# Transposed attention scores from high and low fp16 parts of query and key, with the low part subtracted on GpSimd

## The reference

```python
h = rms_norm(layernorm(x), norm_weight)          # x is [32, 256, 128]
q, k, v = split(h @ w_qkv.T, 3)                  # 16 heads of 64
q, k = apply_rope(q), apply_rope(k)
k = concat([persist_mem, k], axis=2)             # 4 keys in front: 260
v = concat([persist_mem, v], axis=2)
scores = einsum('bhid,bhjd->bhij', q, k) * dim_head ** -0.5
attn = softmax(where(causal, scores, min), -1)
x = x + einsum('bhij,bhjd->bhid', attn, v) @ w_out.T
c = in_c                                         # [256, 128]
for xt in layernorm(x):                          # 32 steps, one sequence each
    f, i = sigmoid(xt @ wf.T + c @ uf.T + bf), sigmoid(xt @ wi.T + c @ ui.T + bi)
    c = f * c + i * tanh(xt @ wc.T + c @ uc.T + bc)
out = x + tanh(layernorm(x) @ wo.T + c @ uo.T + bo)
```

## Time and profile before

| | before |
|---|---|
| median of 3 runs | 1352.43 us |
| lowest and highest | 1346.96 and 1360.31 us |
| profiled execution, its own time | 1353.34 us |
| profiled execution, its span | 1351.6 us |
| instructions in the span | 38016 |
| mean granted clock of TensorE | 0.958 |
| TensorE matmul, weight load | 88%, 64% of the span busy |
| VectorE, ScalarE, GpSimd | 75%, 46%, 45% |

### The profile page before, as it was taken

One profiled execution on the slowest core, in us unless ns is written; L12 is line 12 of the kernel. 1 busy time (PEld: TensorE's weight loads), 2 busy tenths in 40 slices (PEclk: granted clock), 3 DMA queues, 4 the chain that ended last, 5 costly groups with the idle time before them and its releaser, 6 DMA issues.

```text
span 1351.6 us, 38016 instructions
## 1 busy us (share of the span) xinstructions
PE 1185.7 (88%) x13841; PEld 868.7 (64%) x13841; DVE 1008.0 (75%) x3415; ACT 625.3 (46%) x1305; POOL 612.1 (45%) x948
## 2 busy tenths in 40 slices
PE   2799999999999999999999999999999999999950
PEld 1467766676776666667666666766666766667640
DVE  3767878787787877778787777877777887787426
ACT  2455444444554544545444454544445454454412
POOL 2445444444454444445444444544444454444204
PEclk9799999999999999999999999999999999999965
DMA  8222333333222323322332332223233322332114
...
DMA packets 72554, 122.63 MB, mean 91 GB/s; under 512 B 12593, under 2 KB 27442, under 8 KB 72242
## 3 DMA queue, kind: packets, MB, share of 16 engines
...
...
## 4 chain that ended last, share of the span: by engine, by line
PE 42%; DMA 18%; DVE 17%; SPq 9%; issue 7%; POOL 4%; ACT 2%; POOLq 0%; DVEq 0%; ACTq 0%
DMA rope_c<-rope_b 12%; PE bank L845 8%; PE bank_pv L935 7%; DVE masked L657 6%; DMA linv_scratch<-linv 5%; PE bank_sum L969 5%; PE bank_sum L952 5%; SPq L258 5%; PE bank_st L898 4%; DVE linv L673 4%; POOL qk L348 3%; PE bank_sm L875 3%; PE bank L861 2%; SPq L243 2%; DVE rope_b L647 2%
## 5 line engine op out<-in xcount | busy, mean ns | idle before, releaser
L348 POOL TENSOR_TENSOR qk<-rope_a,rope_c 128x512 f32<-128x512 f32 x256 | 325.5, 1272 | 413.0 <-DMA rope_c<-rope_b 392.3
L657 DVE CUSTOM_DVE_ANT_0 masked<-bank_sm,mask_q 128x132 bf16<-128x132 f32 (+1 forms) x1024 | 307.4, 356 | 42.8 <-PE bank_sm L875 42.8
L646 DVE TENSOR_TENSOR rope_a<-bank,cos 128x512 f32<-128x512 f32 x256 | 174.6, 682 | 181.4 <-PE bank L845 127.3
L466 ACT ACTIVATE prob<-bank_st 128x776 f32<-128x776 f32 x256 | 208.4, 814 | 158.4 <-PE bank_st L901 157.7
L935 PE MATMUL bank_pv<-prob,v_sb 128*64 128x256 f32 (+1 forms) x2048 | 229.5, 345 | 52.4 <-ACT raw L489 51.4
L451 ACT ACTIVATE qk_h<-qk 128x512 f16<-128x512 f32 x256 | 159.4, 623 | 208.3 <-POOL qk L348 208.1
L898 PE MATMUL bank_st<-qk 64*128 64x256 f32 (+1 forms) x2048 | 240.3, 327 | 0.0
L339 POOL TENSOR_SCALAR_AFFINE_SELECT prob<-prob 128x256 f32<-128x256 f32 x256 | 113.8, 444 | 262.6 <-ACT prob L466 262.3
L935 PEld LDWEIGHTS bank_pv<-prob,v_sb 128*64 128x64 f32 x2048 | 128.9, 137 | 123.5 <-POOL prob L341 55.1
L898 PEld LDWEIGHTS bank_st<-qk 64*128 64x128 f32 x2048 | 155.1, 188 | 31.7 <-issue 1.1
L647 DVE TENSOR_TENSOR rope_b<-bank,sin 128x512 f32<-128x512 f32 x256 | 173.8, 679 | 0.0
...
## 6 DMA issues: line engine op xcount, KB each, us to landing
rope_c<-rope_b SPq DMA_DIRECT2D x512, 128.0 KB, 2.1
rinv<-linv_scratch SPq DMA_DIRECT2D x128, 256.0 KB, 4.5
...
v_sb<-pm_v SPq DMA_DIRECT2D x64, 8.0 KB
...
```

What stands on the lines that cost most here:

```text
L348: G.tensor_tensor(qk[:, s, :].rearrange("p (u n) -> p u n", u=2)[:, :, 0:NT], rope_a[:, s % 4, :].rearrange("p (u n) -> p u n", u=2), rope ...
L466: A.activation(prob[:, s % 4, :, :], ps_st[:, :, 0:SCOL], ACT.Exp).then_inc(S["exp_done"], 1)
L646: V.tensor_tensor(rope_a[:, s % 4, :], ps_proj[:, :], cos[:, :], ALU.mult)
L657: ins = V.tensor_tensor_reduce(masked[:, e, c0:c0 + n], ps_sm[:, e, c0:c0 + n], mask_q[:, c0:c0 + n], 1.0, LOWEST, ALU.add, ALU.max, top[: ...
```

## The change

The transposed scores are no longer one fp32 product but three fp16 ones, (high, high), (high, low) and (low, high), as the projections are already. `qk_h` is there already; its partner `qk_l` is new, the difference of `qk` and `qk_h` in fp16. GpSimd subtracts it in the new `low`, for pair s-2 behind `causal` of turn s (for the last two pairs in turns 0 and 1 of the next iteration). `qk` shrinks to four buffers: `rope_add` waits for `low` of four pairs before, no longer for the scores of the batch before, and ScalarE's cast now waits for these scores. The keys of persistent memory get a low part once, in VectorE's prologue. `k_end` becomes two tiles, `k_end_h` and `k_end_l`, copied one behind the other, and `end_keys` moves from turns 1 and 6 to turns 3 and 7.

```diff
--- before.py
+++ after.py
@@ -109,11 +109,13 @@
 
 
 
-        qk = sb("qk", [P, NPAIR, 2 * NKEY], f32)
-        k_end = sb("k_end", [P, NPAIR * NEND], f32)
+        qk = sb("qk", [P, 4, 2 * NT], f32)
+        k_end_h = sb("k_end_h", [P, NPAIR * NEND], f16)
+        k_end_l = sb("k_end_l", [P, NPAIR * NEND], f16)
         top_t = sb("top_t", [P, 2, NT], bf16)
 
         qk_h = sb("qk_h", [P, NPAIR, 2 * NKEY], f16)
+        qk_l = sb("qk_l", [P, NPAIR, 2 * NKEY], f16)
         v_sb = sb("v_sb", [P, 2, DI], f32)
         v_end = sb("v_end", [P, DI], f32)
 
...
@@ -343,12 +345,18 @@
 
             def rope_add(j, s):
 
+                wait(pool, S["lo_done"], NPAIR * j + s - 3)
+                pool.wait_ge(swapped[s % 2], 32 * (NPAIR // 2 * j + s // 2 + 1))
+                G.tensor_tensor(qk[:, s % 4, :], rope_a[:, s % 4, :], rope_c[:, s % 2, :], ALU.add).then_inc(S["rope_sum"], 1)
+
+            def low(j, s):
+
+                pool.wait_ge(S["hi_done"], NPAIR * j + s + 1)
                 wait(pool, S["st_ready"], NPAIR * (j - 1) + s + 1)
-                pool.wait_ge(swapped[s % 2], 32 * (NPAIR // 2 * j + s // 2 + 1))
-                G.tensor_tensor(qk[:, s, :].rearrange("p (u n) -> p u n", u=2)[:, :, 0:NT],
-                                rope_a[:, s % 4, :].rearrange("p (u n) -> p u n", u=2),
-                                rope_c[:, s % 2, :].rearrange("p (u n) -> p u n", u=2),
-                                ALU.add).then_inc(S["rope_sum"], 1)
+                G.tensor_tensor(qk_l[:, s, :].rearrange("p (u n) -> p u n", u=2)[:, :, 0:NT],
+                                qk[:, s % 4, :].rearrange("p (u n) -> p u n", u=2),
+                                qk_h[:, s, :].rearrange("p (u n) -> p u n", u=2)[:, :, 0:NT],
+                                ALU.subtract).then_inc(S["lo_done"], 1)
 
             def rstd(cj):
 
@@ -368,6 +376,10 @@
                         rstd(j - 2)
                     if b:
                         causal(j - 1, s)
+                    if s < 2 and b:
+                        low(j - 1, NPAIR - 2 + s)
+                    if s >= 2 and a:
+                        low(j, s - 2)
                     if s == 1 and real(j + 1):
                         factors(QT, j + 2, POOL_H * (j + 1))
 
@@ -424,7 +436,6 @@
 
             act.wait_ge(S["ld_small"], 64)
             pk = pmk_raw[:, :].rearrange("p (c n) -> p c n", c=NPAIR)
-            cast(A.copy(qk[:, :, NT:NT + NPM], pk))
             cast(A.copy(qk_h[:, :, NT:NT + NPM], pk))
 
             def late_casts():
@@ -446,10 +457,10 @@
             def hi(j, s):
 
                 act.wait_ge(S["rope_sum"], NPAIR * j + s + 1)
-                wait(act, S["sm_ready"], NPAIR * (j - 1) + s + 1)
+                wait(act, S["st_ready"], NPAIR * (j - 1) + s + 1)
 
                 A.activation(qk_h[:, s, :].rearrange("p (u n) -> p u n", u=2)[:, :, 0:NT],
-                             qk[:, s, :].rearrange("p (u n) -> p u n", u=2)[:, :, 0:NT], ACT.Copy).then_inc(S["hi_done"], 1)
+                             qk[:, s % 4, :].rearrange("p (u n) -> p u n", u=2), ACT.Copy).then_inc(S["hi_done"], 1)
 
             def exp(bj, s):
                 act.wait_ge(S["st_ready"], NPAIR * bj + s + 1)
@@ -467,10 +478,13 @@
 
             def end_keys(j, half):
 
-                act.wait_ge(S["rope_sum"], NPAIR * j + 4 * half + 4)
+                act.wait_ge(S["lo_done"], NPAIR * j + 4 * half + 4)
+                act.wait_ge(S["hi_done"], NPAIR * j + 4 * half + 4)
                 wait(act, S["st_ready"], NPAIR * (j - 1) + 4 * half + 1)
-                A.activation(k_end[:, half * KE:half * KE + KE].rearrange("p (s n) -> p s n", n=NEND),
-                             qk[:, 4 * half:4 * half + 4, NKEY + QE:NKEY + NT], ACT.Copy).then_inc(S["k_end_done"], 1)
+                for dst, src in ((k_end_h, qk_h), (k_end_l, qk_l)):
+                    ins = A.activation(dst[:, half * KE:half * KE + KE].rearrange("p (s n) -> p s n", n=NEND),
+                                       src[:, 4 * half:4 * half + 4, NKEY + QE:NKEY + NT], ACT.Copy)
+                ins.then_inc(S["k_end_done"], 1)
 
             def copy_top(j, half):
 
@@ -541,9 +555,9 @@
                         hi(j - 1, NPAIR - 1)
                     if s >= 1 and a:
                         hi(j, s - 1)
-                    if s == 1 and b:
+                    if s == 3 and b:
                         end_keys(j - 1, 1)
-                    if s == 6 and a:
+                    if s == 7 and a:
                         end_keys(j, 0)
                     if s == 0 and c:
                         raw_copy(j - 2, p, NPAIR - 1)
@@ -617,6 +631,9 @@
             V.scalar_tensor_tensor(w_lo[:, 0:2 * DI], w_raw[:, 0:2 * DI], WS, w_hi[:, 0:2 * DI], ALU.mult,
                                    ALU.subtract).then_inc(S["casts_dve"], 1)
             dve.wait_ge(S["ld_rope"], 32)
+            dve.wait_ge(S["casts_act"], 8)
+            V.tensor_tensor(qk_l[:, :, NT:NT + NPM], pmk_raw[:, :].rearrange("p (c n) -> p c n", c=NPAIR),
+                            qk_h[:, :, NT:NT + NPM], ALU.subtract).then_inc(S["casts_dve"], 1)
 
             def end_low():
                 dve.wait_ge(S["end_hi"], 1)
...
@@ -887,16 +904,19 @@
                 if isinstance(bj, int) and bj == 0 and s == 0:
                     pe.wait_ge(S["ld_small"], 64)
                     pe.wait_ge(S["ld_wo"], 16)
-                    pe.wait_ge(S["casts_act"], 12)
+                    pe.wait_ge(S["casts_act"], 11)
                     pe.wait_ge(S["ve_copied"], 2)
                 if s % 4 == 0:
                     pe.wait_ge(S["top_copied"], 2 * bj + 1 + s // 4)
 
                 wait(pe, S["exp_done"], NPAIR * bj + s)
+                QK = (qk_h, qk_l)
+                pe.wait_ge(S["lo_done"], NPAIR * bj + s + 1)
                 for kc, q0, c0 in CHUNKS:
-                    for e in range(2):
-                        T.matmul(ps_st[:, e, c0:c0 + NT - q0], qk[OWN[e], s, NT + kc * P:NT + (kc + 1) * P],
-                                 qk[OWN[e], s, q0:NT], start=True, stop=False)
+                    for i, (p, q) in enumerate(SPLIT):
+                        for e in range(2):
+                            T.matmul(ps_st[:, e, c0:c0 + NT - q0], QK[p][OWN[e], s, NT + kc * P:NT + (kc + 1) * P],
+                                     QK[q][OWN[e], s, q0:NT], start=(i == 0), stop=False)
                     for e in range(2):
                         last = T.matmul(ps_st[:, e, c0:c0 + NT - q0], sel_shift[OWN[e], s, :],
                                         top_t[OWN[e], s // 4, q0:NT], start=False, stop=True)
@@ -907,9 +927,11 @@
                     pe.wait_ge(S["k_end_done"], 2 * bj + half + 1)
                     T.sem_inc(S["pe_tick"], 1)
                     out_end = [ps_st[32 * half:32 * half + KE, e, SCOL:SCOL + KE] for e in range(2)]
-                    for e in range(2):
-                        T.matmul(out_end[e], k_end[OWN[e], half * KE:half * KE + KE], qk[OWN[e], s:s + 4, QE:NT],
-                                 start=True, stop=False)
+                    KEND = (k_end_h, k_end_l)
+                    for i, (p, q) in enumerate(SPLIT):
+                        for e in range(2):
+                            T.matmul(out_end[e], KEND[p][OWN[e], half * KE:half * KE + KE], QK[q][OWN[e], s:s + 4, QE:NT],
+                                     start=(i == 0), stop=False)
                     for e in range(2):
                         T.matmul(out_end[e], sel_end[OWN[e], s:s + 4, :].rearrange("p s n -> p (s n)"),
                                  top_t[OWN[e], half, QE:NT].unsqueeze(1).to_broadcast([64, 4, NEND]),
...
```

8 lines of the change are left out of this document (4 added, 4 removed).

## The result

The changed kernel takes 1377.67 us in the median of four runs (1376.14 to 1382.88), the kernel before 1349.70 beside it (1344.22 to 1360.31). The ratio is 1.020, with a 95% interval of 1.0156 to 1.0244: slower beyond the noise, by about 2%; whether by more or by less than 2% the interval leaves open. The forecast was 1358 and no change that counts, so its likeliest case did not come. The time lies in the stated range, 1338 to 1386, and within 2 us of the third rival (the port, 1379). The profiled execution took 1376.32 us, its span is 1374.6, 23.0 more than before.

The account below looks back on a forecast made before the run. The prediction took a cycle of TensorE's own work (half A) and a fixed latency (half B) as the bound. Its terms, -8.4 + 6.6 + 1.5 + 3 + 3.4 = +6.1 us, gave 1358 us, range 1338 to 1386.

Parts of the forecast that it names:

- the third rival: Slower by the port: VectorE's second division held up to 0.8 us per iteration, +24 us, 1379 us; chance 0.13.
- the port: SBUF interfaces shared by GpSimd and VectorE: the subtraction holds the second division, 0.1 us per iteration, +3 us.
- half A: TensorE's own work in the cycle, from pair 3's values through turns 5, 6, 7, 0 to turn 1's scores for the maxima.
- The first rival: Faster: TensorE is the bound and all 36 us come off, 1317 us; chance 0.14 together with its milder form.
- its milder form: Half B's waits, split by L969, no longer bring the low clock: 20 us off, 1338; chance 0.14 with the first rival.
- The second: Slower: the longer wait before L935 brings the low clock every iteration, 31 us instead of 3.4, 1386 us; chance 0.17.
- The fourth: Slower: the subtraction costs near 2.5 us, GpSimd has no slack and TensorE pays, 1400 us or more; chance 0.05.
- Scores: TensorE's transposed scores: 0.14 us saved a pair (0.12 or 0.16), counting only in turns 7 and 0, -8.4 us.
- The end keys: ScalarE's two copies behind the cast lengthen half B by 0.22 us per iteration, +6.6 us; TensorE's small matmuls wait, +1.5.
- The subtraction: GpSimd's new subtraction takes 1.27 us like its addition, 325 us more in all, hidden by its idle time.
- Clock: TensorE's low clock after long waits: two more stretches of 3.4 us, each 1.7 us dear, +3.4 us.
- half B: Fixed latency from turn 1's maxima through inverse sums, pair 2's swap, addition, cast and copy to pair 3's values.

Follow-up runs that it names:

- skip6: Changed kernel with the subtraction of pair 4 moved from turn 6 to turn 7, nothing else: 1345.33 us, ratio 0.9964.
- grouped: Changed kernel with four of the eight subtractions together in turn 2, the others in turns 4, 5, 7 and 0: 1351.59 us, ratio 0.999.
- sub_only: Kernel before plus GpSimd's subtraction at the change's places, its result never read: 1368.45 us, ratio 1.0146.
- no_sub: Changed kernel with GpSimd's subtraction cut to two of 256 columns, the other low parts zero from the prologue on: 1352.57 us, ratio 0.9998.
- swap_first: Changed kernel with pair 4's subtraction in turn 7, end-key copies before the cast, pair 2's swap issued before the inverse sums' read-back: 1284.71 us, ratio 0.9495.
- keys_only: Kernel before with two fp32 end-key copies instead of one, in the changed kernel's places: 1359.7 us, ratio 1.0046.
- swap_before: Kernel before with only SyncE's order changed: swap of pair 2 between store and read-back of the inverse sums: 1291.78 us, ratio 0.9541.
- swap_grouped: swap_first with the subtractions placed as in grouped, four of them in turn 2: 1296.82 us, ratio 0.9585.

## What of the prediction failed and what held, point by point

**The step that failed** is the port, +3 us in the sum. Its mechanism was named, and its price was read from the right rows, but only for the divisions of turn 4. Their hold came as described, and larger: they take 1092 ns, not 865, and two of them 3.02 us, not 2.07. VectorE and GpSimd of the kernel after:

```profile
778.88 3.02 DVE L699 TENSOR_TENSOR raw<-rinv,raw 128x512 f32<-128x512 f32 x2
```
```profile
778.51 1.16 POOL L356 TENSOR_TENSOR qk_l<-qk,qk_h 128x512 f16<-128x512 f32 x1
779.63 1.72 POOL L350 TENSOR_TENSOR qk<-rope_a,rope_c 128x512 f32<-128x512 f32 x1
```

and it cost half A nothing, as skip6 and grouped show together; the 0.1 us per iteration was even too much.

What the step left out is every other place at which a subtraction now stands beside VectorE. The measured term is 0.85 us of half A per iteration (after less skip6; 0.76 in sub_only), 25 us, eight times the +3, and it is `xn` in turn 6. That instruction had 330 ns in the median before, 510 after, and no wait of TensorE hung on it but twice; no row and no term of the prediction has it. It should have been found: in the order of GpSimd the subtraction of turn 6 is one of eight, and the cast of `c_hi`, which the prediction named as lying on the chain, was there to see with the same sickness. In the kernel before it takes 1.32 us beside an addition; in the prologue, with no instruction of GpSimd beside it, the same cast takes 293 ns. VectorE and GpSimd before:

```profile
699.17 1.32 DVE L742 CAST c_hi<-c 128x256 f16<-128x256 f32 x1
...
L638 DVE CAST c_hi<-c 128x256 f16<-128x256 f32 x1 | 0.3, 293 | 0.0
```
```profile
699.07 1.27 POOL L348 TENSOR_TENSOR qk<-rope_a,rope_c 128x512 f32<-128x512 f32 x1
```

**The rivals.** The time is that of the third, and its mechanism is right: the port. Its place is not. It had the second division held for 0.8 us per iteration at TensorE's expense; in fact the divisions were held for (1092 - 865) x 4 = 0.9 us and nobody waited, and the 0.85 us came at `xn`. That +24 and +25 agree is luck. A chance of 0.13 was too low for a unit of which 296 us of new work were put beside VectorE's 1000. The first rival (TensorE is the bound) fell with no_sub: that kernel has 37 us less of TensorE than the kernel before (1148.8 us) and the same time; its milder form fell with the 51.2 us of low clock. The second (the clock in every iteration) did not come: the low clock comes to 15 stretches of 3.4 us in the 28 iterations, 11 before. The fourth fell with the 1158 ns.

**Scores.** Right, near the upper of the two values. TensorE after, a pair's two chunks:

```profile
775.83 0.27 PE L918 MATMUL bank_st<-qk_h 64*128 64x256 f16 x2
...
776.16 0.27 PE L921 MATMUL bank_st<-top_t,sel_shift 64*128 64x256 bf16 x2
776.26 0.22 PE L918 MATMUL bank_st<-qk_h 64*128 64x132 f16 x2
776.32 0.22 PE L918 MATMUL bank_st<-qk_l,qk_h 64*128 64x132 f16 x2
776.38 0.22 PE L918 MATMUL bank_st<-qk_h,qk_l 64*128 64x132 f16 x2
776.44 0.22 PE L921 MATMUL bank_st<-top_t,sel_shift 64*128 64x132 bf16 x2
```

Three products of 256 columns take 0.33 us (775.83 to 776.16) and three of 132 take 0.18 (776.26 to 776.44), where the fp32 product took 0.43 and 0.23: 0.15 us a pair, and the values of the next pair start 0.16 us sooner (5.37 us behind those of pair 3, not 5.53, in the mean of the iterations without a low clock).

What reaches half A was forecast as 0.28 us. no_sub shows 0.20 and skip6 0.37. That the forecast lies between them is in part luck, for the split by turns was not right. In no_sub the values of turn 7 start 0.21 us sooner after those of turn 4 than before, but the scores for the maxima in turn 0, behind them, only 0.05, so that turn 7's saving is lost again; turn 0's own brings the 0.20. The trace of swap_first has a gap there before the value projection, and its chain leads that to VectorE's `xt_lo`. What skip6 has beyond no_sub comes in turns 6 and 7 and goes, as I read it, back to the cast of `c_hi`: 1044 ns in no_sub, 923 in skip6, and the wait before the maxima is transposed is 26.7 us in 27 iterations in the one, 21.8 in 31 in the other, 18.6 in 27 before. In the kernel after a cast starts at 788.44 and ends with the subtraction before the addition, 0.79 us; the one of 699.17 in the kernel before starts with the addition and takes 1.32. The subtraction helps here by chance and harms at `xn`. No run tests this reading by itself.

**The end keys.** Right. ScalarE after:

```profile
777.86 0.63 ACT L462 ACTIVATE qk_h<-qk 128x512 f16<-128x512 f32 x1 [6.35 <-POOL qk L350]
778.39 0.20 ACT L485 ACTIVATE k_end_h<-qk_h 128x16 f16<-128x16 f16 x1
778.50 0.20 ACT L485 ACTIVATE k_end_l<-qk_l 128x16 f16<-128x16 f16 x1
778.61 0.36 ACT L503 ACTIVATE raw<-bank_pv 128x256 f32<-128x256 f32 x1
```

From cast to copy it is 0.75 us, 0.54 before: +0.21, forecast 0.22, and 6.3 us in keys_only. The small matmuls wait for `k_end_l` and start at 778.85, those on the values at 779.11, 0.50 us behind the copy, which is the 0.51 of before. The +1.5 us is nearer to zero.

**The subtraction** takes 1158 ns, under the 1270 that I took. GpSimd comes to 917.9 us, forecast 937. It has no idle time before it, and the swaps still end 240.6 us of GpSimd's idle time, so that the engine as such is no bound.

**Clock.** Right in size, as far as one profile each can tell. In half A there are 46.4 - 37.0 = 9.4 us more at the low level, +4.7 us, forecast 3.4; with half B it is 13.7 us more, four stretches where two were forecast, but the mean of half B is only 0.03 us higher with the iterations that have one in it than without them. The count varies between executions of one kernel: the mean granted clock of the four executions of the kernel after goes from 0.950 to 0.958, that of sub_only from 0.959 to 0.971. So the 16.6 us of sub_only's profile, with nearly the same wait before the values as the kernel before, are in part such scatter, and it follows no simple rule of the waits in half B. What sets it is open. What is shown is the far end: where the wait before the values is gone, half A has no low clock (the three swap kernels), and what is left in half B is none (swap_before), 6.8 us (swap_first) and 10.2 (swap_grouped).

**Where the sum went**, for 30 iterations, forecast and measured: scores -8.4 and -6 to -11; copies +6.6 and +6.3 (but half B as a whole only +0.14 x 30 = +4.2); end-key matmuls +1.5 and about 0; port +3 and +25; clock +3.4 and +4.7, the last from one profile each. Four of five terms were good to 3 us or so, and the fifth decided.
